# Padding the rows of the activation buffers in a four-block transformer kernel: 16 bytes after each row of act0, 8 bytes after each row of act1

## The chip, the cores and the metric

The kernel runs on one core of one Trainium2 chip. The metric is device time in microseconds (us). A core has five engines that run side by side and meet through semaphores: TensorE (PE, matrix products), VectorE (DVE), ScalarE (ACT), GpSimd (POOL) and SyncE (SP, which here issues the transfers). SBUF is the on-chip memory of 128 partitions; an address below is a byte offset inside one partition. TensorE reads two operands from it: the stationary one is loaded ahead of each matmul by a weight load (PEld in the profile), the moving one is streamed through column by column.

## The reference, cut to what matters

16 sequences of 512 tokens and 256 features pass through four sublayers, each with a residual: linear attention (A), a gated feed-forward net (B), softmax attention (C) and a tanh layer. The change touches only B:

```python
def _L0_ffn_ref(x, w1_w, w1_s, w2_w, w2_s, h1_w, h1_s, h2_w, h2_s, w3_w, w3_s):
    h = jax.nn.silu(_tlin(x, w1_w, w1_s)) * _tlin(x, w2_w, w2_s)     # 256 -> 1024
    h = jax.nn.gelu(_tlin(h, h1_w, h1_s), approximate=False)         # 1024 -> 1024
    h = jax.nn.gelu(_tlin(h, h2_w, h2_s), approximate=False)         # 1024 -> 1024
    return _tlin(h, w3_w, w3_s)                                      # 1024 -> 256
x = x + _L0_ffn_ref(_layernorm(x, axis=-1), ...)
```

The weights of B are ternary, so they are exact in the reduced format float32r. An activation is not: it is kept as two float32r parts, hi (the rounded value) and lo (what the rounding left), and every product with it is made twice, once per part.

## The kernel before

A sequence is worked in two halves of 256 tokens (HT) in the feed-forward net. An activation of 1024 features and 256 tokens is stored as eight blocks of 128 features: a buffer is `[128 partitions, KH = 8, HT = 256]` of 4 bytes, so in each partition it is eight rows of 1024 bytes, one behind the other. There are four such buffers: act0_hi, act0_lo, act1_hi, act1_lo. The steps of one half are named in the program's tables and run in this order on TensorE, with attention steps of the neighbouring sequences (names with c: and a:) woven in by orders written out by hand:

- U0 to U3: w1 and w2 products from half_hi and half_lo. Each step makes two blocks of act0: ACT does silu, DVE the scaled product (`whole`, L793), DVE rounds it into act0_hi (L798), POOL subtracts to give act0_lo (L649).
- G0 to G3: h1 products. act0 is the moving operand, h1 the stationary one (L1117). ACT does gelu and the rounding into act1_hi (L980), DVE the subtraction into act1_lo (L802).
- H0 to H3: h2 products, the same with act1 read and act0 written.
- W0, W1: w3 products (L1174). Here act0 is the stationary operand, in pieces of 128 tokens, and w3 the moving one.

Each G or H step is 32 matmuls: for each row k of eight, for each of two output blocks, one with act_hi and one with act_lo, 256 columns each, with its own weight load:

```python
for k in halves(piece, KH):
    if j == 0 and k % 2 == 0:
        pe.wait_ge(s["ffn_ready"], c.value("ffn_ready", k // 2 + 1 - PAIRS))
    for o in range(2):
        w = weights[:, k, (2 * j + o) * P:(2 * j + o + 1) * P]
        for half, moving in enumerate((act_hi[src], act_lo[src])):
            last = pe.matmul(two(bank)[:, o, :], view(w), view(moving[:, k, :]), ...)
```

So there are 32 halves, in each 128 matmuls of G and 128 of H: 8192 in all that stream a row of act0 or act1. W has 1024.

SBUF is given out in the order of the listing. Of the compiled program before, these are the first bytes of the tensors that the text speaks of, with the remainder by 128:

```
w12 1152 (0)      h1 17536 (0)       h2 50304 (0)       w3 83072 (0)      wkv_hi 95360 (0)   wvo_hi 109696 (0)
half_hi 144224 (96)   act0_hi 148320 (96)   act1_hi 156512 (96)   act0_lo 164704 (96)   act1_lo 172896 (96)
xt_hi 193376 (96)   qz_hi 201568 (96)   m_parts 213856 (96)   staged (holds values_hi and prob_t) 217952 (96)
late_xt, late_qz (laid over w12 and h1 for the last sequence): remainder 0
```

All rows of all these tensors are multiples of 512 bytes long, so every row of a tensor has its tensor's remainder. The tensor `rows`, which holds the bias rows, begins at 118092, 12 bytes past a multiple of 16.

Of the kernel before, what the change touches and what calls it, by code (L numbers as in the profile page):

```python
# [28 lines left out]
F32R = mybir.dt.float32r  # L29
# [6 lines left out]
P = 128  # L36
# [3 lines left out]
KH = HID // P  # L40
# [4 lines left out]
HT = S // 2  # L45
# [6 lines left out]
LOOK = 2048  # L52
SQUARED = 1024
SQ = 32

# [244 lines left out]
def build(nc, a):  # L302
    with ExitStack() as ctx:
        def sb(name, shape, dt=F32):
            return ctx.enter_context(nc.sbuf_tensor(name, shape, dt))
# [39 lines left out]
        xn_b = sb("xn_b", [P, HB, D])  # L345
        half_hi = sb("half_hi", [P, KD, HT], F32R)
        half_lo = sb("half_lo", [P, KD, HT], F32R)
        act0_hi = sb("act0_hi", [P, KH, HT], F32R)
        squares_at = -(-nc.sbuf_base // 32) * 32
        act_hi = [act0_hi, sb("act1_hi", [P, KH, HT], F32R)]  # L350
        early_squares = nc.alloc_sbuf_tensor_at("early_squares", [P, SQUARED], F32, offset=squares_at)
        act_lo = [sb(f"act{n}_lo", [P, KH, HT], F32R) for n in range(2)]
        gated = sb("gated", [P, 2, 2, HT])
        whole = sb("whole", [P, WHOLES, 2, HT])
        w_tmp = xn_b
# [118 lines left out]
        def wait(eng, which, value):  # L474
            if value is not None and not (isinstance(value, int) and value <= 0):
                eng.wait_ge(which, value)
# [190 lines left out]
        def _(dve):  # L667
# [21 lines left out]
            def part(step, c, slots, share=""):  # L689
# [66 lines left out]
                elif kind == "T":  # L756
# [3 lines left out]
                    wait(dve, s["xt_lo_ready"], c.value("xt_lo_ready"))  # L760
                    for there in range(P // 2 if share == "b" else 0, P // 2 if share == "a" else P, SQ):
                        for here in range(0, P, SQ):
                            into = turned[there:there + SQ].rearrange("p k (b n) -> p b k n", b=NB)
                            last = dve.transpose(into[:, :, :, here:here + SQ],  # L764
                                                 own.xn[here:here + SQ].rearrange("p b (k n) -> p b k n", k=KD)
                                                 [:, :, :, there:there + SQ])
                    if share != "a":
# [601 lines left out]
```

## Time and profile before

| | |
|---|---|
| time, median of 3 runs | 1981.3 us (1980.95 to 1983.38) |
| span of the profiled execution | 1981.5 us, 37810 instructions |
| mean granted TensorE clock | 0.996 of full speed |
| TensorE busy | 1961.9 us, 15288 matmuls |
| TensorE weight loads busy | 1895.6 us |
| VectorE, ScalarE, GpSimd busy | 1289.0, 1020.0, 406.8 us |

The span runs from the first to the last instruction of the profiled execution; it is within 0.2 us of the median of the runs. Matmuls overlap in the profile (one is in flight for about 280 ns, and the next starts after less than half of that), so what a stream of them costs is read from the distance between starts, or from the length of a piece of the chain divided by its count.

### The profile page before, as it was taken

What the parts mean: (1) busy time and instruction counts of PE and PEld (TensorE: products, weight loads), DVE (VectorE), ACT (ScalarE), POOL (GpSimd) and SP (SyncE); (2) the same over time, 40 slices, a digit from 0 to 9 for tenths busy, and PEclk for the clock granted to TensorE, in tenths of its full rate; (3) what the DMA queues carried; (4) which work ended last, traced back from release to release, by engine and by line L of the source; (5) the groups of instructions that cost most, each with busy time, mean ns of one, the idle gap of its engine ahead of it and who ended that gap; (6) DMA issues with size and microseconds to landing.
All of it is one profiled execution on the core that took longest, in us unless ns stands there. A gap on an engine that the chain in (4) does not pass through costs nothing.

```text
span 1981.5 us, 37810 instructions
## 1 busy us (share of the span) xinstructions
PE 1961.9 (99%) x15288; PEld 1895.6 (96%) x15288; DVE 1289.0 (65%) x3292; ACT 1020.0 (51%) x1786; POOL 406.8 (21%) x344
## 2 busy tenths in 40 slices
PE   8999999999999999999999999999999999999998
PEld 7999999999999999999999999999999999999996
DVE  6546768566685665767667676666856667676357
ACT  3445545555554655455554455555546454554433
POOL 1112212212122021311213121121220213112121
PEclk9999999999999999999999999999999999999999
DMA  9600000000000000000000000000000000000000
GB/s 359 224 3 1 22 1 12 11 2 22 1 22 1 1 22 1 22 1 1 22 1 22 1 1 22 1 22 1 23 1 1 22 1 12 1 1 12 1 1 23
DMA packets 24538, 46.03 MB, mean 23 GB/s; under 512 B 1264, under 2 KB 21488, under 8 KB 24176
## 3 DMA queue, kind: packets, MB, share of 16 engines
q1 hardware_dynamic: 24352, 43.41, 6.1%
q8 instruction: 134, 2.20, 0.5%
q14 instruction: 52, 0.43, 0.1%
HBM read 35.02 MB, written 19.92 MB: 28 GB/s over the span
## 4 chain that ended last, share of the span: by engine, by line
PE 97%; DMA 1%; DVE 1%; SPq 1%; issue 0%; ACT 0%; POOL 0%; DVEq 0%; ACTq 0%
PE ffn_fill L1117 49%; PE att_fill L1048 25%; PE ffn_fill L1048 13%; PE ffn_fill L1174 6%; PE att_fill L1136 1%; PE att_fill L1252 1%; DMA scratch_w2T<-in_w2T 1%; DMA w<-scratch_w1T 0%; SPq L543 0%; PE ffn_fill L1285 0%; DVE late_sm L869 0%; PE ffn_fill L1280 0%; ACT late_kv_b L1009 0%; DVE st L671 0%; DVE late_prob_t_lo L864 0%
## 5 line engine op out<-in xcount | busy, mean ns | idle before, releaser
L1117 PE MATMUL ffn_fill<-act_hi,h 128*128 128x256 f32 x4096 | 987.2, 283 | 0.8 <-issue 0.2
L1117 PE MATMUL ffn_fill<-act_lo,h 128*128 128x256 f32 x4096 | 978.2, 280 | 1.2 <-issue 1.2
L1117 PEld LDWEIGHTS ffn_fill<-act_hi,h 128*128 128x128 f32 x4096 | 770.3, 188 | 9.2 <-POOL act_lo L649 3.9
L1117 PEld LDWEIGHTS ffn_fill<-act_lo,h 128*128 128x128 f32 x4096 | 773.1, 189 | 3.6
L976 ACT ACTIVATE whole<-ffn_fill,scales 128x256 f32<-128x256 f32 x512 | 214.0, 469 | 291.3 <-PE ffn_fill L1117 290.1
L649 POOL TENSOR_TENSOR act_lo<-whole,act_hi 128x512 fp32r<-128x512 f32 x128 | 166.8, 1303 | 492.4 <-DVE act_hi L798 492.4
L802 DVE TENSOR_TENSOR act_lo<-whole,act_hi 128x512 fp32r<-128x512 f32 x256 | 183.4, 716 | 112.0 <-ACT act_hi L980 109.7
L1048 PE MATMUL ffn_fill<-half_hi,w 128*128 128x256 f32 x1024 | 245.9, 283 | 0.0
L1048 PE MATMUL ffn_fill<-half_lo,w 128*128 128x256 f32 x1024 | 244.3, 281 | 0.0
L1048 PEld LDWEIGHTS ffn_fill<-half_lo,w 128*128 128x128 f32 x1024 | 193.3, 189 | 0.1
L1048 PEld LDWEIGHTS ffn_fill<-half_hi,w 128*128 128x128 f32 x1024 | 192.5, 188 | 0.4 <-issue 0.2
L631 POOL TENSOR_TENSOR rstd_B<-var_eps_B,minus_half 128x2 f32<-128x2 f32 x32 | 27.8, 868 | 776.4 <-DVE var_eps_B L680 776.4
L967 ACT ACTIVATE gated<-ffn_fill,scales 128x256 f32<-128x256 f32 x256 | 107.3, 471 | 140.4 <-PE ffn_fill L1048 137.3
L980 ACT ACTIVATE act_hi<-whole 128x512 fp32r<-128x512 f32 x256 | 161.9, 633 | 8.1
L976 ACT ACT_TABLE_LOAD x102 | 130.9, 1283 | 59.7 <-PE ffn_fill L1117 58.7
L779 DVE STREAM_TRANSPOSE turned_b<-xn_b 32x128 f32<-32x128 f32 x464 | 140.4, 303 | 6.5
L793 DVE SCALAR_TENSOR_TENSOR whole<-ffn_fill,scales,gated 128x256 f32<-128x256 f32 x256 | 111.8, 478 | 50.3 <-PE ffn_fill L1048 29.3
L1174 PE MATMUL ffn_fill<-w,act_hi 128*128 128x256 f32 x512 | 121.2, 280 | 0.0
L1174 PE MATMUL ffn_fill<-w,act_lo 128*128 128x256 f32 x512 | 120.9, 279 | 0.0
L764 DVE STREAM_TRANSPOSE turned<-xn 32x256 f32<-32x256 f32 x224 | 97.5, 435 | 2.9
L1174 PEld LDWEIGHTS ffn_fill<-w,act_lo 128*128 128x128 f32 x512 | 96.5, 188 | 0.0
L671 DVE BATCH_NORM_STATS2 st<-x 128x6 f32<-128x256 f32 x252 | 92.7, 415 | 5.8 <-DMA x<-in_L_attn_x 4.3
(239 smaller groups left out, 3277.8 us busy)
## 6 DMA issues: line engine op xcount, KB each, us to landing
x<-in_L_attn_x SPq DMA_DIRECT2D x16, 512.0 KB, 3.3
out<-x SPq DMA_DIRECT2D x15, 512.0 KB, 2.9
h<-scratch_h1T SPq DMA_DIRECT2D x2, 2048.0 KB, 13.1
h<-scratch_h2T SPq DMA_DIRECT2D x2, 2048.0 KB, 13.4
w<-scratch_w1T SPq DMA_DIRECT2D x1, 1024.0 KB, 7.8
w<-scratch_w2T SPq DMA_DIRECT2D x1, 1024.0 KB, 9.8
w<-scratch_w3T SPq DMA_DIRECT2D x1, 1024.0 KB, 8.3
rows<-in_rows SPq DMA_DIRECT2D x1, 640.0 KB, 5.5
```

Source lines behind the costliest of these rows:

```text
L649: pool.tensor_tensor(act_lo[0][:, blocks], whole[:, n % WHOLES], act_hi[0][:, blocks].bitcast(F32), ALU.subtract).then_inc(s["ffn_ready"], 1)
L671: last = dve.bn_stats(st[:, b, :], xs[:, b, :])
L764: last = dve.transpose(into[:, :, :, here:here + SQ], own.xn[here:here + SQ].rearrange("p b (k n) -> p b k n", k=KD) [:, :, :, there:there ...
L779: last = dve.transpose(into[:, :, :, here:here + SQ], xn_b[here:here + SQ].rearrange("p b (k n) -> p b k n", k=KD) [:, :, :, there:there + ...
L793: last = dve.scalar_tensor_tensor(whole[:, n % WHOLES, o, :], two(bank)[:, o, :], scales[:, 1, 2 * j + o:2 * j + o + 1], gated[:, j % 2, o ...
L802: dve.tensor_tensor(act_lo[dst][:, blocks], whole[:, n % WHOLES], act_hi[dst][:, blocks].bitcast(F32), ALU.subtract).then_inc(s["ffn_ready ...
L967: last = act.activation(gated[:, j % 2, o, :], two(bank)[:, o, :], ACT.Silu, scale=scales[:, 0, 2 * j + o:2 * j + o + 1])
L976: last = act.activation(whole[:, n % WHOLES, o, :], two(bank)[:, o, :], ACT.Gelu, scale=scales[:, layer, 2 * j + o:2 * j + o + 1])
L980: act.activation(act_hi[1 if kind == "G" else 0][:, 2 * j:2 * j + 2], whole[:, n % WHOLES], ACT.Copy)\
L1048: last = pe.matmul(out, lhsT, rhs, start=n == 0, stop=n == len(pairs) - 1)
L1117: last = pe.matmul(two(bank)[:, o, :], view(w), view(moving[:, k, :]), start=k == 0 and o == 0 and half == 0, stop=k == KH - 1 and half == ...
L1174: last = pe.matmul(bank[:, 0:D], view(part_of[:, k, b * P:(b + 1) * P]), view(w3[:, k, :]), start=k == 0 and half == 0, stop=k == KH - 1 a ...
```

## The change

Each of the four buffers is allocated with a longer row and used through a slice that leaves the extra elements out. The row of act0_hi and act0_lo becomes 260 elements (1040 bytes), that of act1_hi and act1_lo 258 (1032 bytes). Nothing reads or writes the padding.

```diff
+ROW_PAD = (4, 2)
...
-        act0_hi = sb("act0_hi", [P, KH, HT], F32R)
+        act0_hi = sb("act0_hi", [P, KH, HT + ROW_PAD[0]], F32R)[:, :, :HT]
         squares_at = -(-nc.sbuf_base // 32) * 32
-        act_hi = [act0_hi, sb("act1_hi", [P, KH, HT], F32R)]
+        act_hi = [act0_hi, sb("act1_hi", [P, KH, HT + ROW_PAD[1]], F32R)[:, :, :HT]]
         early_squares = nc.alloc_sbuf_tensor_at("early_squares", [P, SQUARED], F32, offset=squares_at)
-        act_lo = [sb(f"act{n}_lo", [P, KH, HT], F32R) for n in range(2)]
+        act_lo = [sb(f"act{n}_lo", [P, KH, HT + ROW_PAD[n]], F32R)[:, :, :HT] for n in range(2)]
```

After it act0_hi begins at 148320 (remainder 96), act1_hi at 156640 (96), act0_lo at 164896 (32) and act1_lo at 173216 (32); everything allocated behind them moves up by 384 bytes, three times 128, and keeps its remainder. Row k of act0 lies 16k bytes further by the remainder, row k of act1 8k.

No instruction is added, dropped or moved on any engine. What changes is the form of those that write two rows at once. On VectorE, in the second half of a sequence (U1 to U3 of the loop's body, then the first products of G; `whole` is the product before rounding), the rows of the program before are:

```order
191 L798 CAST act_hi<-whole 128x512
192 L793 SCALAR_TENSOR_TENSOR whole<-ffn_fill,scales,gated 128x256 x2
193 L798 CAST act_hi<-whole 128x512
194 L754 TENSOR_TENSOR xt_lo<-att_fill,xt_hi 128x2x2x128 x2
195 L793 SCALAR_TENSOR_TENSOR whole<-ffn_fill,scales,gated 128x256 x2
196 L798 CAST act_hi<-whole 128x512
202 L802 TENSOR_TENSOR act_lo<-whole,act_hi 128x512 x2
```

and of the changed program at the same place, where each line number is one higher because of the added line:

```order
191 L799 CAST act_hi<-whole 128x2x256
192 L794 SCALAR_TENSOR_TENSOR whole<-ffn_fill,scales,gated 128x256 x2
193 L799 CAST act_hi<-whole 128x2x256
194 L755 TENSOR_TENSOR xt_lo<-att_fill,xt_hi 128x2x2x128 x2
195 L794 SCALAR_TENSOR_TENSOR whole<-ffn_fill,scales,gated 128x256 x2
196 L799 CAST act_hi<-whole 128x2x256
202 L803 TENSOR_TENSOR act_lo<-whole,act_hi 128x2x256 x2
```

Nothing moved; the write of 512 elements in one run has become two runs of 256 with a gap between them. The same holds for L980 on ScalarE and L649 on GpSimd.

## Rows read from the trace of the kernel before

**Rows 1.** Page, part 1: busy time of each engine

```profile
PE 1961.9 (99%) x15288; PEld 1895.6 (96%) x15288; DVE 1289.0 (65%) x3292; ACT 1020.0 (51%) x1786; POOL 406.8 (21%) x344
```

**Rows 2.** Page, part 4: shares of the chain that ended last

```profile
PE 97%; DMA 1%; DVE 1%; SPq 1%; issue 0%; ACT 0%; POOL 0%; DVEq 0%; ACTq 0%
```

**Rows 3.** Page, part 5: matmul and weight-load groups of the feed-forward net

```profile
L1117 PE MATMUL ffn_fill<-act_hi,h 128*128 128x256 f32 x4096 | 987.2, 283 | 0.8 <-issue 0.2
L1117 PE MATMUL ffn_fill<-act_lo,h 128*128 128x256 f32 x4096 | 978.2, 280 | 1.2 <-issue 1.2
L1117 PEld LDWEIGHTS ffn_fill<-act_hi,h 128*128 128x128 f32 x4096 | 770.3, 188 | 9.2 <-POOL act_lo L649 3.9
```

**Rows 4.** Chain in order of time, 700 to 812 us: start, us, what

```profile
702.40 13.25 PE ffn_fill L1117 x112
715.65 5.60 PE att_fill L1048 x24
...
732.39 2.86 PE att_fill L1048 x24
735.25 9.46 PE ffn_fill L1117 x80
744.71 3.73 PE ffn_fill L1174 x32
748.44 7.57 PE ffn_fill L1048 x64
756.01 2.84 PE ffn_fill L1117 x24
758.85 0.01 issue
758.86 3.10 PE ffn_fill L1117 x24
...
777.84 2.76 PE att_fill L1048 x12
...
797.16 1.44 PE att_fill L1048 x12
```

**Rows 5.** Groups by shape, TensorE: one product at two places in SBUF

```profile
L1048 PE MATMUL att_fill<-wvo_hi,xt_hi 128*128 128x256 f32 x120 | 33.5, 279 | 0.0
...
L1048 PE MATMUL ffn_fill<-wvo_hi,late_xt_hi 128*128 128x256 f32 x8 | 2.2, 281 | 0.0
```

**Rows 6.** Instructions on act_hi: ns min/median/max, who waited

```profile
L980 ACT ACTIVATE act_hi<-whole x256: 630/632/636, 67.5 to 1916.7; 128x512 fp32r<-128x512 f32 x128
L802 DVE TENSOR_TENSOR act_lo<-whole,act_hi x256: 673/686/1241, 71.3 to 1917.3; 128x512 fp32r<-128x512 f32 x128
L798 DVE CAST act_hi<-whole x128: 426/428/843, 48.8 to 1885.2; 128x512 fp32r<-128x512 f32 x128
L649 POOL TENSOR_TENSOR act_lo<-whole,act_hi x128: 1273/1293/1394, 49.3 to 1885.7; 128x512 fp32r<-128x512 f32 x128
```

**Rows 7.** Single lines with operands in pieces: ns min/median/max

```profile
L754 DVE TENSOR_TENSOR xt_lo<-att_fill,xt_hi x64: 679/682/693, 10.4 to 1966.1; 128x512 fp32r<-128x512 f32 x64
L949 ACT ACTIVATE xt_hi<-att_fill x64: 578/597/608, 9.1 to 1965.3; 128x512 fp32r<-128x512 f32 x64
L626 POOL TENSOR_TENSOR x<-x,rows x64: 1267/1292/1752, 22.3 to 1929.3; 128x512 f32<-128x512 f32 x64
```

**Rows 8.** Timeline, 757 to 759 us: last pair of U, first half

```profile
757.02 0.43 DVE L798 CAST act_hi<-whole 128x512 fp32r<-128x512 f32 x1
...
757.52 1.29 POOL L649 TENSOR_TENSOR act_lo<-whole,act_hi 128x512 fp32r<-128x512 f32 x1 [0.59 <-DVE act_hi L798]
```

## Prediction

> **What bounds the kernel now.** I read the busy times first, then the chain of what ended last, then that chain in order of time. TensorE is busy for 1961.9 of 1981.5 us [rows 1] and makes 97% of the chain [rows 2]; the granted clock is 0.996 of full speed, so practically all of it runs at 2.4 GHz. VectorE, at 65%, is the next engine. So an edit counts here in two ways only: it changes the pace at which TensorE's matmuls follow each other, or it makes an operand late enough that TensorE stands still. The room for the second is small: the weight loads for act_hi stood idle 9.2 us in all, 3.9 of it put down to GpSimd's act_lo [rows 3]. So the question is the pace.
>
> The pace is not one number. From the pieces of the chain [rows 4], dividing length by count:
>
> - G, 112 matmuls in 13.25 us: 118.3 ns. H, 80 in 9.46 us: 118.3 ns. U, 64 in 7.57 us: 118.3 ns. In all three the moving operand has remainder 96 by 128 bytes and the stationary one 0.
> - W, 32 in 3.73 us: 116.6 ns. Here moving is 0 and stationary 96.
> - Key and value products of A (wkv moving, 0; xt stationary, 96), 24 of 512 columns in 5.60 us: 233.3 ns, or 116.7 per 256 columns.
> - Last products of A (m_parts moving against qz, both 96), 24 in 2.86 us: 119.2 ns. Output of C (values against prob_t, both 96), 12 in 1.44 us: 120.0 ns.
> - Scores of C (xt moving against qz, both 96), 12 of 512 columns in 2.76 us: 230 ns, or 115.0 per 256 columns. That is the quickest of these.
>
> 256 columns at 2.4 GHz are 106.7 ns, so each matmul of G and H gives away 11.6 ns, and other groups of the same size and format give away more or less. The groups differ in what they multiply, too, so this alone doesn't show that addresses matter. One product occurs at two addresses: wvo with xt (remainders 0 and 96) has a mean of 279 ns, wvo with late_xt (0 and 0) 281 [rows 5]. Since a matmul's time in the profile grows with the distance to the next, this speaks for a small effect of place, about 2 ns, but on 8 instances only.
>
> **The change part by part.** No instruction is added or moved. Three things change.
>
> First, the rows that TensorE streams in G and H: 8192 matmuls, each of whose nanoseconds costs 8.19 us. Today every such row stands at 96 by 128 bytes, every weight row at 0. Afterwards the rows of act0_hi go through 96, 112, 0, 16, ... 80, those of act0_lo through 32, 48, ... 16: each step of 16 bytes occurs once. Those of act1 go in steps of 8 from 96 (hi) and 32 (lo). The trace has no row at these places, so the price is bounded by the groups above. Lower end: all take the 115.0 ns of the scores, 3.3 ns less, −27 us. Upper end: all take the 120.0 ns of C's output, +14 us. Nearest are the arrangements in which the two operands stand apart, W and the key and value products, at 116.6; the one in which they stand together gives 119.2 to 120.0, and that should now come up at one row in eight. Seven parts of 116.6 and one of 120.0 are 117.0 ns: 1.3 ns less than now, times 8192 is −10.6 us. I take that.
>
> Second, W loads act0 rows as stationary operand, in pieces of 512 bytes that now begin at other remainders: 1024 matmuls, at 116.6 now. Between 115.0 and 120.0 this is −1.6 to +3.5 us. I take 0, since W is already at the level that I expect of the others.
>
> Third, the writers write two runs of 256 instead of one of 512. Other instructions of this trace already work in pieces: VectorE's xt_lo, whose output is in runs of 128, takes 682 ns (median) against 686 for act_lo; ScalarE's xt_hi, also in runs of 128, takes 597 against 632 for act_hi; GpSimd's bias addition, whose second operand is one row read twice and begins 12 bytes past a multiple of 16, takes 1292 against 1293 for its act_lo [rows 6, 7]. So these cost nothing. The exception may be VectorE's rounding, L798: 428 ns for 512 elements, where the subtraction over as many takes 686 [rows 6]. It runs in some faster form that no row shows in two runs. If it lost that, it would take about 686, +258 ns. What is queued behind it is GpSimd's subtraction, and behind that TensorE at the seventh row of G0. In a sequence's first half nothing else stands between U and G: the last rounding ends at 757.45, the subtraction behind it at 758.81 [rows 8], and TensorE, which had done 24 matmuls (six rows) from 756.01 to 758.85, goes on at 758.86 and needs 3.10 us for the next 24 instead of 2.84 [rows 4]. So there every nanosecond of the rounding is exposed: 258 ns at 16 first halves, +4.1 us. In the second half a piece of other products stands in the middle of G0 and gives room. I take 0.
>
> The Trainium skill ("VectorE: DVE Perf Modes", Mode 2×_2P) says a copy within SBUF is split along its outermost dimension over two read ports, if that is even in source and destination. 428 against 686 ns agrees, and 512 and 2 are both even, so by it the form is kept; the sum would be the same.
>
> Sum: −10.6 + 0 + 0 = −10.6 us against the profiled 1981.5, 1970.9. The median of the runs is 0.2 lower. I say **1971 us**.
>
> **The rivals.**
>
> *Nothing happens.* The pace belongs to the form of the matmul and the order hi, lo, hi, lo, and not to addresses; the padding is then invisible. For it: G, H and U share 118.3 ns though they read different tensors, and these three alone have the order of one weight block used twice, by hi and by lo; what sets the levels is then this pattern. Against it: the two ns of rows 5. Time: 1981.3, and with W and the rounding within 1 or 2 us of it. The Trainium skill takes this side: by "SBUF — State Buffer", Who interferes with whom, TensorE has one read port for the moving operand and an independent one for weight loads and never waits for anyone. By that page no address could matter, and the trace agrees only in that the pace is untouched by how busy the others are.
>
> *It gets slower.* One mechanism: a row that does not begin at a whole line or bank costs an extra step to fetch, or meets the weight load more often. Place: the moving rows of L1117, above all act1's odd rows, 8 bytes off a multiple of 16, which only H reads. Price: if H and G go to the level of C's output, 1.7 ns × 8192 = +14 us, 1995; if only H does, +7 us, 1988. It decides once the mean of the 8192 is above 118.8 ns (4 us / 8192 = 0.5 ns above now). For it: no row in the trace streams from such an address, so nothing excludes it. Against: twelve bytes off did GpSimd no harm.
> The Trainium skill ("Advanced Engine Details and Errata", SBUF Cachelines) speaks of lines of 16 bytes and a penalty when an access crosses to a new one. A row of 1024 bytes that begins 8 off touches 65 lines and not 64; as an estimate from that page this is 1.5% of 2048 of H's matmuls, near +4 us.
>
> *It gets much faster.* The 96 against 0 arrangement is a bad one and most others are near the scores' 115.0 ns or below: 1981.3 − 27 = 1954, and below, if the pace falls nearer to 106.7.
>
> **How the numbers follow.** A timing of this kernel can tell about 0.2% (4 us) from no change. Chances: my forecast, a gain of 4 to 20 us, 0.43; much faster 0.10; nothing 0.27; slower 0.20. So faster 0.53, same 0.27, slower 0.20. The time is the likeliest case's, 1971; its own range is 1962 to 1977. For the whole I leave out the far half of "much faster" and the far part of "slower": 1956 to 1989.
>
> **What would show it.** In the profile after, the pieces of G and H in the chain: 112 matmuls should take 13.1 us instead of 13.25, and mean times of L1118 (L1117 plus the added line) should fall by 1 to 2 ns; U, which is not touched, should stay at 118.3. If G (16-byte steps) and H (8-byte steps) part, alignment below 16 bytes matters. L799 should stay at 428 ns and GpSimd's subtraction at 1293. If the pace is 118.3 as now and the time too, the nothing-case is right; if L799 takes 690 and the weight loads wait longer on act_lo, the third part was mispriced; if act0's pace is above 118.8, the slower rival is right. I am most likely to be wrong in the price of the first part, which rests on a likeness between groups and not on one row at the new addresses.

## The result, and the profile after

The changed kernel takes 1989.15 us (median of 7 runs, 1987.63 to 1989.31), the kernel before, timed beside it, 1983.38 us (1980.95 to 1984.76). The ratio is 1.0029, with a 95% interval of 1.0018 to 1.0039. It is slower by about 6 us; I had said 1971. Its profiled execution has a span of 1986.5 us against 1981.5.

The group of the page that answers to the weight loads of [rows 3] (busy us, mean ns of one, then idle time before them):

```profile
L1118 PEld LDWEIGHTS ffn_fill<-act_hi,h 128*128 128x128 f32 x4096 | 772.5, 189 | 10.8 <-POOL act_lo L650 4.1
```

The waits hardly changed: 4.1 us of the weight loads' idle time are put down to GpSimd's act_lo, against 3.9. The place to look is again the chain in order of time, here of the changed kernel, over one sequence (start, us, what; x112 is G; x80 and all pieces of L1118 from 788 to 809 us are H; L1175 is W):

```profile
704.89 13.19 PE ffn_fill L1118 x112
...
737.69 9.55 PE ffn_fill L1118 x80
747.24 3.79 PE ffn_fill L1175 x32
...
788.36 1.93 PE ffn_fill L1118 x16
...
792.17 1.91 PE ffn_fill L1118 x16
...
796.00 3.86 PE ffn_fill L1118 x32
...
801.28 7.63 PE ffn_fill L1118 x64
808.91 3.78 PE ffn_fill L1175 x32
...
825.86 13.19 PE ffn_fill L1118 x112
```

The same view of the kernel before, those pieces of H and W that [rows 4] did not show, and the start of the next G:

```profile
785.75 1.89 PE ffn_fill L1117 x16
...
789.52 1.89 PE ffn_fill L1117 x16
...
793.38 3.79 PE ffn_fill L1117 x32
...
798.60 7.57 PE ffn_fill L1117 x64
806.16 3.73 PE ffn_fill L1174 x32
...
823.03 13.25 PE ffn_fill L1117 x112
```

From one G to the next a sequence took 120.63 us (702.40 to 823.03) and now takes 120.97 (704.89 to 825.86): +0.34 us, times 16 sequences +5.4, close to the +5.0 of the spans. The pieces say where. H's five pieces of x80 and from 785 us on were 9.46 + 1.89 + 1.89 + 3.79 + 7.57 and are 9.55 + 1.93 + 1.91 + 3.86 + 7.63, +0.28 us; one more H piece, x16, went from 1.89 to 1.91. W's two pieces went from 3.73 to 3.79 and 3.78, +0.11. G's x112 piece fell from 13.25 to 13.19, its others moved by 0.01 at most, −0.07 in sum. H +0.30, W +0.11, G −0.07 make the +0.34. The rest of this sequence is not in it. Summed over the whole trace, from each matmul's start to the next one's, it comes out alike: H 489.7 us before and 494.2 after, W 119.7 and 121.2, G 492.3 and 492.6, where G's sum holds pauses in the first sequence that are 1.9 us longer after.

Within H the odd rows of act1 stand out, those that begin 8 bytes off a multiple of 16. This is the mean distance between starts in steps H2 and H3, over all 32 halves, 1024 matmuls each (worked out from the traces, ns):

| | even rows | odd rows |
|---|---|---|
| kernel before, all rows at 96 by 128 | 119.1 | 117.5 |
| changed kernel, odd rows 8 bytes off | 118.3 | 120.3 |

The odd rows were the quicker ones before and are the slower ones now. The writers, against [rows 6], did not change with their new form:

```profile
L799 DVE CAST act_hi<-whole x128: 426/428/832, 48.2 to 1890.8; 128x512 fp32r<-128x512 f32 x128
L650 POOL TENSOR_TENSOR act_lo<-whole,act_hi x128: 1272/1294/1403, 48.7 to 1891.4; 128x512 fp32r<-128x512 f32 x128
```

### The profile page after: what moved, and what is told of

Same layout as the page of the kernel before. It is cut to its first block, busy times and chain, and to the rows that moved or that the text cites. A ratio compares the mean times of both kernels' runs of the same rounds, so it can differ in the third digit from the quotient of the medians.

```text
span 1986.5 us, 37810 instructions
## 1 busy us (share of the span) xinstructions
PE 1965.7 (99%) x15288; PEld 1900.5 (96%) x15288; DVE 1288.8 (65%) x3292; ACT 1019.7 (51%) x1786; POOL 406.8 (20%) x344
## 4 chain that ended last, share of the span: by engine, by line
PE 96%; DVE 1%; DMA 1%; SPq 1%; issue 0%; ACT 0%; POOL 0%; DVEq 0%; ACTq 0%
PE ffn_fill L1118 49%; PE att_fill L1049 25%; PE ffn_fill L1049 13%; PE ffn_fill L1175 6%; PE att_fill L1137 1%; PE att_fill L1253 1%; DMA scratch_w2T<-in_w2T 1%; DMA w<-scratch_w1T 0%; SPq L544 0%; PE ffn_fill L1286 0%; DVE late_sm L870 0%; ACT late_kv_b L1010 0%; DVE st L672 0%; DVE late_prob_t_lo L865 0%; DVE prob_t_lo L865 0%
## 5 line engine op out<-in xcount | busy, mean ns | idle before, releaser
L1118 PE MATMUL ffn_fill<-act_hi,h 128*128 128x256 f32 x4096 | 989.7, 283 | 2.6 <-issue 1.9
L1118 PE MATMUL ffn_fill<-act_lo,h 128*128 128x256 f32 x4096 | 981.4, 281 | 1.0 <-issue 1.0
L1118 PEld LDWEIGHTS ffn_fill<-act_hi,h 128*128 128x128 f32 x4096 | 772.5, 189 | 10.8 <-POOL act_lo L650 4.1
L1118 PEld LDWEIGHTS ffn_fill<-act_lo,h 128*128 128x128 f32 x4096 | 772.7, 189 | 3.5
L1175 PE MATMUL ffn_fill<-w,act_hi 128*128 128x256 f32 x512 | 122.7, 281 | 0.0
L1175 PE MATMUL ffn_fill<-w,act_lo 128*128 128x256 f32 x512 | 122.5, 281 | 0.0
L1175 PEld LDWEIGHTS ffn_fill<-w,act_lo 128*128 128x128 f32 x512 | 96.4, 188 | 0.0
```

Of the source, the lines that this page charges most:

```text
L1175: last = pe.matmul(bank[:, 0:D], view(part_of[:, k, b * P:(b + 1) * P]), view(w3[:, k, :]), start=k == 0 and half == 0, stop=k == KH - 1 a ...
```

## The experiments

Theory A: a moving row that begins 8 bytes off a multiple of 16 slows its matmul, and the changed kernel has such rows in act1 alone. The rival, theory B: what costs is that the rows walk through the 128-byte places against the weights, whatever the step. In all runs G's pace is read from the piece x112, H's from x64 (a sequence's first half) or x80 (its second), W's from x32 of its line, all in the chain in order of time. Where a sum over the whole trace is given, it is that of the distances from each matmul's start to the next one's; the trace is of one execution. All kernels are the one before except for where things stand in SBUF.

### Other paddings

`pad_4_4` and `pad_4_0` and `pad_0_2` change one line of the changed kernel:

```diff
-ROW_PAD = (4, 2)
+ROW_PAD = (4, 4)      # pad_0_2: (0, 2), pad_4_0: (4, 0)
```

**Both 16 bytes.** 

> Both act0 and act1 rows get 16 bytes; all rows now begin at a multiple of 16 bytes. Theory A (a moving row that begins 8 bytes off a multiple of 16 costs about 2.4 ns a matmul): H falls back from 119.5 to about 118 ns, its total from 494.2 to about 490 us, the W cost of +1.5 us stays, time about 4.5 us below the changed kernel, near +0.1% of before. Theory B (what costs is that rows walk through the 128-byte phases against the weights, whatever the step): H stays at 119 ns or above, time as the changed kernel or slower.

Measured: 1983.19 us, ratio 0.9998 [0.9989, 1.0007]. The chain:

```profile
703.39 13.27 PE ffn_fill L1118 x112
...
799.61 7.50 PE ffn_fill L1118 x64
807.11 3.76 PE ffn_fill L1175 x32
```

H at 117.2 ns, quicker than before (118.3) and than the changed kernel (119.2). Rows that walk in steps of 16 bytes cost H nothing; theory B falls. W costs +0.03 us a piece.

**Act1 alone.** 

> Only act1 gets its 8 bytes. Theory A: H at 119.5 ns (+4.5 us), G and W as before; about 1.0023 of before. Theory B: the same H, but rows at even k (16-byte multiples) slower as well as odd ones. If the cost was in act0's padding, H is at 118.3 and the time that of before.

Measured: 1989.71 us, ratio 1.0034 [1.0021, 1.0047].

```profile
736.30 9.51 PE ffn_fill L1118 x80
...
799.85 7.60 PE ffn_fill L1118 x64
```

The kernel is slower with the 8-byte padding alone, but H's share is smaller than I had expected (118.8 ns, half of the rise). Summed over the trace H is +1.7 us, where I had said +4.5, while G and W make −0.3 and all other matmuls and pauses +3.6, of which one pause of 1.3 us at 55 us is part. So this ratio by itself says little of act1; the place of the later tensors, another one here, is a candidate for the rest, and I did not separate it. The rows say more: in H2 and H3 the even ones, at multiples of 16, take 117.5 ns and the odd ones 120.1. Theory B wanted the even ones slow too.

**Act0 alone.** 

> Only act0 gets its 16 bytes. Theory A: G and H at 118 ns, only W (act0 as stationary operand) at 118.2 instead of 116.7, +1.5 us; about 1.0008 of before. Theory B: H, which reads unpadded act1 rows, as before too; G, whose rows walk, no slower than before since it wasn't in the changed kernel.

Measured: 1980.17 us, ratio 0.9982 [0.9972, 0.9991]. Neither theory had this.

```profile
701.96 13.17 PE ffn_fill L1118 x112
...
797.94 7.46 PE ffn_fill L1118 x64
805.40 3.81 PE ffn_fill L1175 x32
```

H reads unpadded rows here, as before, and goes at 116.6 ns instead of 118.3. Act0's padding has moved act1_hi and act1_lo by different amounts: the lo rows now stand 16384 + 128 bytes behind the hi rows. W pays +0.08 us a piece. So there is a second effect of place, as large as the first, at multiples of 16 bytes.

### Where the buffers begin, without padding

These runs leave the rows 1024 bytes apart and move only the first byte. In `start_A_B` each of the four buffers gets 128 bytes of room at its end, act0 is used from byte A on and act1 from byte B:

```diff
+        def shifted(name, first):
+            flat = sb(name, [P, KH * HT + 32], F32R)
+            return flat[:, first:first + KH * HT].rearrange("p (k n) -> p k n", k=KH)
...
-        act0_hi = sb("act0_hi", [P, KH, HT], F32R)
+        act0_hi = shifted("act0_hi", 0)
...
-        act_hi = [act0_hi, sb("act1_hi", [P, KH, HT], F32R)]
+        act_hi = [act0_hi, shifted("act1_hi", 2)]
...
-        act_lo = [sb(f"act{n}_lo", [P, KH, HT], F32R) for n in range(2)]
+        act_lo = [shifted(f"act{n}_lo", (0, 2)[n]) for n in range(2)]
```

**Act1 8 bytes further.** 

> Rows stay 1024 bytes apart, but both act1 buffers begin 8 bytes further, so that all eight rows, not four, begin 8 bytes off a multiple of 16, and none walks through the phases. Theory A: all of H's 4096 matmuls pay about 2.4 ns, H about +10 us, time about 1.005 of before. Theory B (walking costs): H as before, time within 0.1% of before.

Measured: 2001.54 us, ratio 1.0088 [1.0073, 1.0102]: +17 us.

```profile
710.51 13.25 PE ffn_fill L1121 x112
...
736.74 4.11 PE ffn_fill L1121 x32
...
743.72 9.60 PE ffn_fill L1121 x80
...
807.68 7.68 PE ffn_fill L1121 x64
```

G, whose rows are untouched, stays at 118.3. H is at 120.0 ns in its long pieces and at 128 in the x32 one. Nothing walks here, and the loss is three times that of the changed kernel and larger than the 1.005 that I had expected. Most of it is in such slow stretches: summed over the trace, H0 and H1 are +13.6 us, H2 and H3 +4.6.

**Act1 16 bytes further.** 

> The layout of the run whose act1 began 8 bytes further, but with 16 bytes: all rows at multiples of 16. Theory A (only the part below 16 bytes costs): H between 116.7 and 118.5 ns, time within 0.2% of before. Rival (any shift of the moving row away from 96 by 128 costs): H at 120 ns or more as with 8 bytes, ratio near 1.009.

Measured: 1969.97 us, ratio 0.9927 [0.9912, 0.9943].

```profile
729.45 9.11 PE ffn_fill L1121 x80
...
792.36 7.30 PE ffn_fill L1121 x64
...
816.66 13.24 PE ffn_fill L1121 x112
```

Another 8 bytes, and H is at 114.1 ns, quicker than anything in the kernel before, which was below the 116.7 to 118.5 that I had allowed. From 8 to 16 bytes the kernel gains 32 us. These two runs have the same layout in all else.

With H this quick, W meets a wait that the kernel before did not have. In a sequence's first half its piece takes 3.88 us (at 799.66), in the second 3.74. Timeline:

```profile
801.59 0.69 DVE L806 TENSOR_TENSOR act_lo<-whole,act_hi 128x512 fp32r<-128x512 f32 x1
...
802.20 0.27 PE L1178 MATMUL ffn_fill<-w,act_lo 128*128 128x256 f32 x1
...
802.33 0.19 PEld L1178 LDWEIGHTS ffn_fill<-w,act_hi 128*128 128x128 f32 x1
802.34 0.38 PE L1178 MATMUL ffn_fill<-w,act_hi 128*128 128x256 f32 x1
```

VectorE finishes act0's last two rows at 802.28, and W, which needs them for the matmul at 802.34, loads at 802.33 and stands 0.14 us from the matmul before and 0.22 from the next, where 0.117 is its usual step; over the trace W is +1.6 us, though act0 kept its place by 256 bytes.

**Act1 24 and 32 bytes further.** 

> The same layout again, act1 beginning 24 bytes further, again 8 off a multiple of 16. Theory A (8 off 16 costs wherever it is): H at 120 ns or more, like the run with 8 bytes and unlike that with 16, ratio 1.003 to 1.01. Rival (each place has its own level and 16 was merely lucky): anything between 113 and 122.

 

> Act1 begins 32 bytes further, so hi and lo rows are at multiples of 32, as in the kernel before. Theory E (a moving row that begins 16 off a multiple of 32, while the weight rows begin at multiples of 32, goes at 114 ns; one at a multiple of 32 at 117 to 118): H at 117 to 118.5, time within 0.3% of before. Rival (any 16-byte multiple in this layout gives 114, from the distance of 16640 bytes between hi and lo): H at 114, ratio 0.993.

Measured: 1992.69 us, ratio 1.0045 [1.0029, 1.0060], and 1986.32 us, ratio 1.0007 [0.9998, 1.0017]. With 24 bytes:

```profile
800.84 7.74 PE ffn_fill L1121 x64
```

and with 32:

```profile
800.23 7.59 PE ffn_fill L1121 x64
```

120.9 and 118.6 ns: 8 off a multiple of 16 is slow again, and the next multiple of 16 is back at the usual level, so 16 is not quick as such.

**Act0 8 bytes further.** 

> The same layout, act0 instead of act1 begins 8 bytes further: G streams all its rows from there, and W loads them as stationary operand. Theory A: G goes to 120 ns or more, at least +7 us, with up to +18 us as H had; H as before. W tells whether the stationary operand pays as well: 116.7 ns if not, near 120 (+3 us) if so. The rival that act1 is special: G stays at 118.3.

Measured: 1993.36 us, ratio 1.0044 [1.0029, 1.0060].

```profile
703.36 13.44 PE ffn_fill L1121 x112
...
799.99 7.66 PE ffn_fill L1121 x64
```

G goes to 120.0 ns, as theory A says. The half of it on H was wrong: H should have stayed at 118.3 and is at 119.7. Its buffers begin at a multiple of 32, but the room added to act0 has moved them by 128 bytes, from 96 to 224 by 256. W, which loads act0 as stationary operand, went from 3.73 to 3.77 us a piece and not to the 120 ns that I had named if it paid as well.

**Both 16 bytes further, and U's operand too.** 

> Both act0 and act1 begin 16 bytes further. Theory E: G goes to 114 ns as H did, together 8192 x 4.1 ns = -33 us at most, W unknown within 3 us; ratio near 0.985. Rival (the gain belongs to act1's place alone): G stays at 118.3, ratio near 0.993.

 

> The same and also half_hi and half_lo, the moving operand of U, 16 bytes further. Theory E: U from 118.3 to 114 ns, 2048 x 4.3 = -9 us more than the run with act0 and act1 alone. Rival: U unchanged at 243.8 us in sum.

Measured: 1968.89 us, ratio 0.9920 [0.9906, 0.9934], and 1966.74, ratio 0.9916 [0.9903, 0.9930]. With act0 and act1:

```profile
914.45 7.30 PE ffn_fill L1121 x64
...
938.73 13.13 PE ffn_fill L1121 x112
```

and with half_hi and half_lo as well (x64 is U):

```profile
741.06 7.55 PE ffn_fill L1055 x64
```

G gains 1.1 ns and not 4, U next to nothing. Theory E, by which 16 off a multiple of 32 is quick, falls.

### What picks the level at multiples of 16

**A gap behind the buffers.** The kernel before with 384 bytes behind act1_lo:

```diff
+        sb("spare", [P, 96])
         gated = sb("gated", [P, 2, 2, HT])
```

> The kernel before with 384 unused bytes behind act1_lo: all later tensors stand where the changed kernel has them, act0 and act1 where they were. If the later tensors' place cost part of the +5 us, it shows here as attention products slower by 0.5 us or more in sum; I expect G, H, W at 118.3, 118.3, 116.7 ns and a time within 0.1% of before.

Measured: 1985.85 us, ratio 1.0003 [0.9993, 1.0012].

```profile
703.50 13.25 PE ffn_fill L1118 x112
...
799.75 7.57 PE ffn_fill L1118 x64
```

G and H are those of before. The later tensors' new place costs nothing that the timing resolves; in the one profiled execution everything outside G, H, U and W was 2.9 us longer.

**Lo 128 bytes further from hi.**

```diff
+        sb("spare", [P, 32])
         act_lo = [sb(f"act{n}_lo", [P, KH, HT], F32R) for n in range(2)]
```

> The kernel before with 128 unused bytes between act1_hi and act0_lo and no padding: every lo row stands 16384 + 128 bytes behind its hi row instead of 16384. In the run that padded act0 alone, H read unpadded rows at just this distance and went at 116.9 ns instead of 118.3. If the distance of the hi row from the lo row sets the level (theory D), G and H both go to about 116.7 ns: 8192 x 1.5 ns = -12 us, ratio 0.994. If that run's H was quicker for another reason (what the place of act1 or of the tensors behind it does), G and H stay at 118.3 and the time that of before within 0.2%.

Measured: 1977.97 us, ratio 0.9963 [0.9949, 0.9976].

```profile
794.78 7.47 PE ffn_fill L1118 x64
802.25 3.78 PE ffn_fill L1175 x32
819.18 13.07 PE ffn_fill L1118 x112
```

116.7 ns in both G and H, as expected. The gain of 7 us is less than my 12: W pays 0.05 us a piece again, though no row of act0_hi moved and all rows are multiples of 32. Over the trace G and H are −10.9 us, W +1.3 and the attention's and other products +1.1; part of the difference I can't place.

**The place by 256.** In the runs with H at 114 ns act1 stood at 240 by 256 bytes, while act0 beside it in the run with both 16 further stood at 112, and G was at 117.2. The weights h1 and h2 stand at 128 by 256. So the next two kernels put 128 spare bytes ahead of act0, give each buffer 256 bytes of room, and begin all four at 240 by 256, or act1 at 112:

```diff
+        sb("spare", [P, 32])
+        act0_hi = shifted("act0_hi", 4, 64)
...
+        act_hi = [act0_hi, shifted("act1_hi", 4, 64)]      # place_240_112: 36 instead of 4
...
+        act_lo = [shifted(f"act{n}_lo", (4, 4)[n], 64) for n in range(2)]      # (4, 36)
```

> All four buffers unpadded, all beginning 240 by 256 bytes, where act1 stood in the runs whose H went at 114 ns (act0 stood at 112 by 256 there, and G at 117.4). Theory F (the level belongs to the place by 256, the weights standing at 128 by 256): G goes to 114 ns too, -13 us beside the run with both 16 bytes further, time near 1955 to 1960, ratio 0.985 to 0.988. Rival (the level is act1's or H's own, or comes from the distances between buffers): G stays at 117 to 118.3, ratio near 0.992.

 

> The same layout, act1 128 bytes further, at 112 by 256. Theory F: G at 114 ns, H back at 117.4 ns. Rival (H's own): H stays at 114.

Measured: 1961.24 us, ratio 0.9884 [0.9868, 0.9901], and 1971.89, ratio 0.9939 [0.9922, 0.9956]. All at 240:

```profile
727.32 9.10 PE ffn_fill L1122 x80
736.42 3.84 PE ffn_fill L1179 x32
...
790.11 7.26 PE ffn_fill L1122 x64
...
814.32 12.74 PE ffn_fill L1122 x112
```

Act1 at 112:

```profile
793.95 7.50 PE ffn_fill L1122 x64
...
818.44 12.74 PE ffn_fill L1122 x112
```

G goes to 113.8 ns and, with act1 at 240, H to 113.4; moved by 128 bytes, H is back at 117.2 while G stays. The level belongs to the place and not to the buffer or the step; in the first of these kernels act0 stands at 496 by 512 bytes and act1 at 240, so that a class by 512 is not needed. The time is just above the 1955 to 1960 that I had expected. The kernel with all four at 240 is quicker than the one before by 1.2% (22 us), although W now pays 0.11 us a piece.

## Why the prediction was wrong

**What bounds the kernel: right.** Wherever the span of the profiled execution moved by 5 us or more, the sum of G, H and W over the trace moved the same way, by an amount within 3.2 us of it. Only with act1 alone padded (span +4.9, the sum +1.4) does most of the rise lie elsewhere. The writers set nothing in the changed kernel; in the runs with act1 16 bytes further they did: the wait in W cost about 0.1 us in the first half of a sequence.

**First part, the price of the moved rows: wrong, and this is the failed step.** I priced each row by two levels, 116.6 ns where moving and stationary operand have different remainders by 128 bytes (apart) and 120.0 where they have the same (together), took the mean, and got −10.6 us. Measured from the chain it is G −1.1 and H +4.8 us, +3.7. The two levels did not hold even in the rows that I had: G, H and U stood apart too and went at 118.3, and the scores of C stood together and went at 115.0. Beyond that, two things were wrong in it.

- I let an 8-byte step count as a finer 16-byte step. It does not. The same stream of unpadded rows, all four layouts equal but for act1's first byte, takes (x64 piece by count) 120.0 ns 8 bytes further, 114.1 at 16, 120.9 at 24, 118.6 at 32, and G 120.0 with act0 8 bytes further. Each place 8 off a multiple of 16 was slower than both its neighbours. At the first of them (232 by 256) the long pieces are only 0.3 ns above the 119.7 at 224, but H as a whole takes 507.9 us there against 495.8 at 224 and 475.2 at 240. In the changed kernel half of act1's rows are such, and with 16 bytes in their stead H is at 117.2 instead of 119.2 ns, and the kernel's ratio 0.9998 instead of 1.0029. This I call shown for the direction, for the moving operand. Its exact price isn't one number: it depends on the place too.
- I classed the places by 128 bytes. They differ by 256: at 240 by 256 the stream goes at 113.4 to 114.1 ns, at 112 at 117.2, at 96 at 118.3, at 0 at 118.6, at 224 at 119.7 (hi and lo at the same place each time), and with hi at 96 and lo at 224 at 116.7. The groups that I compared in [rows 4] differ in all of this at once. Against this, the padding of act0 walked its rows through good and bad places, which came out near even: −1.1 us for G. The cleanest pair is that of the last two kernels, where act1 alone moved by 128 bytes and H went from 113.4 to 117.2.

How much of H's +4.8 us is due to the 8 bytes and how much to where the rows begin is not separated by a run. With both padded by 16 bytes act1_hi made the same move from 96 to 224 by 256, and H's x80 and x64 pieces were 0.06 and 0.07 us shorter than before (9.40 and 7.50 against 9.46 and 7.57); but act1_lo began at 224 there and at 160 in the changed kernel, so the two differ in more than the 8 bytes. The rows point to the 8 bytes: odd rows went from 117.5 to 120.3 ns and even ones from 119.1 to 118.3, which for 2048 matmuls each is +5.7 and −1.6 us, if H0 and H1 went like H2 and H3.

**Second part, W: taken as 0, measured +1.8 us,** inside my bounds of −1.6 to +3.5. Act0's place as stationary operand does matter. What rule it follows is open: W rose with act0 padded (3.81), with lo moved by 128 bytes alone (3.78), 8 bytes further (3.77) and at 240 (3.84). With act1's moves it stayed within 3.73 to 3.77, except for the wait told above.

**Third part, the writers: right.** L799 has a median of 428 ns as before, GpSimd's subtraction 1294 against 1293.

**The rivals.** The slower one is nearest to what happened: the place that I had named for it, the 8-byte rows that only H reads, is where the time went, and 1988 us was the forecast for that against 1989.15 measured. That the two are so close is in part luck: I had H at +7 and got +4.8, W added 1.8 and G took off 1.1, and the kernel before was at 1983.38 in this timing and not at 1981.3. My sign for this rival did not come out either: the mean over the 8192 matmuls rose by 0.45 ns (3.7 us) to 118.75, just under the 118.8 that I had set, and act0's pace, which was to be above it, was 117.8. I gave this rival 0.20, because the only evidence on odd addresses that I had was GpSimd's, and another engine's reads say nothing of TensorE's. The Trainium skill ("Advanced Engine Details and Errata", SBUF Cachelines) speaks of a penalty for going to a new 16-byte line, and what I read from it, that a row which begins inside a line costs, has the sign of these runs. The estimate of 1.5% that I worked out from that page is near the difference between 120.9 and 118.6 ns (1.9%) and far from that between 120.0 and 114.1 (5%).

The nothing-case fell with the result, whose interval is clear of 1, and for good with act1 at 8 and at 16 bytes (2001.54 and 1969.97 us). The Trainium skill, "SBUF — State Buffer" (Who interferes with whom), gives TensorE two independent read ports and says that it never waits on another engine; it says nothing of addresses. What I made of it, that no address could matter, does not agree with these runs: place alone moved the pace between 113.4 and 120.9 ns. That this is a collision of the moving read with the weight load is a likely reading, as both are reads by TensorE, but no run moved the weights, so it is not shown.

The much faster case did not come from the padding, but its reading of 96 as a poor place was half right: 112 and 240 were quicker (117.2 and 113.4 ns), 0 and 224 slower.

## What to carry to other kernels

Where TensorE is the bound and streams 4-byte operands, the address of the moving rows is a setting that was worth up to 6% of a matmul here (113.4 against 120.9 ns). Keep every row a multiple of 16 bytes, and don't pad by feel: the three paddings of act0 made its rows walk through good and bad places and left G at 117.6 to 118.5 ns, while one good place, the same for all rows, gave 113.8. Which place is good was found here with the weights at 128 by 256 only. Read the pace as length over count of unbroken pieces of the chain, one group at a time, since an edit that moves one buffer moves all behind it.

## What the runs showed that I had not expected

Moving four buffers to 240 by 256 bytes, with not one instruction changed, took G and H from 118.3 to 113.8 and 113.4 ns a matmul and the kernel from 1983.24 to 1961.24 us. Eight bytes more or less at one buffer's start was worth 32 us (2001.54 against 1969.97). And with act1 8 bytes further one H piece ran at 128 ns a matmul (32 in 4.11 us) while two others at the same addresses ran at 120.0. The starts show two patterns. In H1 of that run they lie 0.12 and 0.14 us apart by turns:

```profile
738.61 0.29 PE L1121 MATMUL ffn_fill<-act_hi,h 128*128 128x256 f32 x1
738.73 0.30 PE L1121 MATMUL ffn_fill<-act_lo,h 128*128 128x256 f32 x1
738.87 0.29 PE L1121 MATMUL ffn_fill<-act_hi,h 128*128 128x256 f32 x1
738.99 0.30 PE L1121 MATMUL ffn_fill<-act_lo,h 128*128 128x256 f32 x1
```

In H2 and H3 of the same run they are 118 to 122 ns apart, 120.6 in the mean. The change from one pattern to the other comes at a break of the stream: in the H0 that begins at 794.23 us the first four rows keep to the quick one; attention products follow, and then the last four rows, 0.20 us from their first start to their second, go by turns at 123 and 137. So at one and the same place the pace also depends on how the stream starts. What picks the pattern is open.
